# Attention stage: turned values copied out by ScalarE, normalised on GpSimd, with another TensorE order

## The reference, cut to what matters

```python
scores = jnp.einsum('bhqd,bhkd->bhqk', q, k) * d ** (-0.5)
attn = jax.nn.softmax(scores, axis=-1) * (s / np.sqrt(s - 1.0))
out = jnp.einsum('bhqk,bhkd->bhqd', attn, v) * s ** (-0.5)
out = jnp.transpose(out, (0, 2, 1, 3)).reshape(b, s, hid)
return out @ w_o.T * hid ** (-0.5)
```

## Time and profile before

| | us |
|---|---|
| median of three runs | 6009.92 (6009.81 to 6016.19) |
| the profiled execution's own time | 6003.23 |
| its span in the trace | 6001.4 |
| attention stage: first product, last normalised pair | 2146.2, 5009.6 |
| loop of 128 pairs, one pair | 22.05 |

### The profile page before, as it was taken

One profiled execution on the slowest core, in us unless ns is written; L12 is line 12 of the kernel. 1 busy time (PEld: TensorE's weight loads), 2 busy tenths in 40 slices (PEclk: granted clock), 3 DMA queues, 4 the chain that ended last, 5 costly groups with the idle time before them and its releaser, 6 DMA issues. The chain is left out here.

```text
span 6001.4 us, 127338 instructions
## 1 busy us (share of the span) xinstructions
PE 5491.4 (92%) x47968; PEld 3697.5 (62%) x47968; DVE 4566.3 (76%) x7538; ACT 3573.0 (60%) x5381; POOL 1569.2 (26%) x2095
## 2 busy tenths in 40 slices
PE   7888846999989979999999999999999996799998
PEld 5666635999977834444444444444444444599998
DVE  6888867555546768888888888888888885756554
ACT  5666633333324547777777777777777776433332
POOL 4666634333320000111111111111111113533332
PEclk9999968999999979999999999999999998899999
DMA  1111194222218921111111111111111112222221
GB/s 49 42 49 49 39 255 123 85 87 84 98 50 295 334 97 44 56 55 57 57 55 56 55 57 58 55 56 55 57 58 55 56 53 89 80 86 87 86 93 52
DMA packets 315519, 495.75 MB, mean 83 GB/s; under 512 B 36314, under 2 KB 221028, under 8 KB 311024
## 3 DMA queue, kind: packets, MB, share of 16 engines
q1 hardware_dynamic: 290544, 425.73, 22.7%
q0 software_dynamic: 24576, 64.56, 3.3%
HBM read 321.82 MB, written 168.82 MB: 82 GB/s over the span
## 5 line engine op out<-in xcount | busy, mean ns | idle before, releaser
L1707 DVE TENSOR_REDUCE at_best<-at_psM 128x2 f32<-128x1024 f32 x2048 | 2409.8, 1219 | 349.3 <-PE at_psM L1751 349.1
L1663 ACT ACTIVATE at_p<-at_psE 128x1024 f32<-128x1024 f32 (+1 forms) x2688 | 2067.9, 819 | 597.5 <-PE at_psE L1767 561.0
L1767 PE MATMUL at_psE<-at_q,at_k 50*128 50x512 f32 x4096 | 1128.4, 428 | 84.8 <-ACT at_p L1663 83.3
L1751 PE MATMUL at_psM<-at_k,at_q 48*128 48x512 f32 x4096 | 1100.1, 455 | 47.5 <-DMA at_v<-scratch_v 26.4
L1777 PE MATMUL at_psO<-at_p,at_v 128*17 128x256 f32 x16384 | 1089.3, 384 | 0.0
L1767 PEld LDWEIGHTS at_psE<-at_q,at_k 50*128 50x128 f32 x4096 | 559.3, 186 | 493.7 <-ACT at_p L1663 246.8
L1088 ACT ACTIVATE e_h_hi<-e_psH 128x512 fp32r<-128x512 f32 x512 | 306.5, 599 | 919.7 <-PE e_psH L90 771.6
L1162 DVE SCALAR_TENSOR_TENSOR e_h_lo<-e_psH,e_h_hi 128x512 fp32r<-128x512 f32 x512 | 353.8, 691 | 601.6 <-ACT e_h_hi L1088 532.5
L1777 PEld LDWEIGHTS at_psO<-at_p,at_v 128*17 128x17 f32 x16384 | 378.0, 97 | 560.5 <-issue 329.3
L1751 PEld LDWEIGHTS at_psM<-at_k,at_q 48*128 48x128 f32 x4096 | 495.1, 187 | 361.0 <-DVE at_best L1707 171.5
L90 PE MATMUL e_psE<-e_w_hi,e_h_hi 128*128 128x256 f32 x2048 | 582.8, 285 | 0.0
(11 more groups left out here) (202 smaller groups left out, 8548.2 us busy)
## 6 DMA issues: line engine op xcount, KB each, us to landing
e_w_raw<-in_w SPq DMA_DIRECT2D x64, 1024.0 KB
scratch_qk<-cp_qkh SPq DMA_DIRECT2D x64, 512.0 KB
scratch_qk<-cp_qkl SPq DMA_DIRECT2D x64, 512.0 KB
at_q<-scratch_qk SPq DMA_DIRECT2D x256, 128.0 KB
at_k<-scratch_qk SPq DMA_DIRECT2D x256, 128.0 KB
scratch_v<-cp_va SPq DMA_DIRECT2D x32, 544.0 KB
at_v<-scratch_v SPq DMA_DIRECT2D x128, 136.0 KB
a_x<-in_x SPq DMA_DIRECT2D x32, 512.0 KB
```

The costliest lines, as they stand in the source:

```text
L1663: nc.scalar.activation(P[:, u:u + n, :], src, ACT.Exp, scale=HD ** -0.5).then_inc(p_ready, 1)
L1707: nc.vector.reduce_max(best[j % 2][:, h, :, qt], psM[h][:], AX_X).then_inc(m_taken, 1)
L1751: last = nc.tensor.matmul(psM[h][:, a, :], Q[j][r, 128 * qt:128 * qt + 128], K[j][r, 512 * h:512 * h + 512], start=True, stop=True)
L1767: last = nc.tensor.matmul(psE[:, u - u0 if n == 2 else 2, :], K[j][r, 128 * kc:128 * kc + 128], Q[j][r, 512 * half:512 * half + 512], star ...
```

## The change

- ScalarE copies the transposed `psO` to a new SBUF tile `TV` (`take_turned`), before the exponential of group 8. `take_values` moves from before group 4 to before group 6.
- VectorE only inverts the sums, from `TV`, behind query unit 8 (`inverse_sums`); before, it inverted and multiplied from PSUM behind unit 5.
- GpSimd multiplies `TV` by the inverses into `O` (`normalise`), between `add_x` and `split_max`.
- Value block 0 waits for `tv_ready` in place of `o_ready`.
- On TensorE most query units stand one place later, and units 14 and 15 stand behind value block 5. The order of keys and values, `turn_values`, `output()` and `turns()` is the same. At the end `project_out` of one slice stands before the last `turn_values`.

The diff, with most of the unchanged lines left out:

```diff
@@ -1458,6 +1458,7 @@
         rden = sb("rden", [128, 2, KC], F32)
+        TV = sb("tv", [128, 2, KC, 32], F32)
         O = sb("o", [128, KC, D], F32)
@@ -1481,7 +1482,7 @@
         xo_done, xo_taken, xo_hi_ready, xo_lo_ready = sem("xo_done"), sem("xo_taken"), sem("xo_hi_ready"), sem("xo_lo_ready")
-        values_clear = sem("values_clear")
+        values_clear, tv_ready = sem("values_clear"), sem("tv_ready")
         wo_done, y_scaled, y_ready = sem("wo_done"), sem("y_scaled"), sem("y_ready")
@@ -1491,7 +1492,7 @@
         LEAD = 6
-        OUT_AT, MAX_AT, VALUES_AT, NORM_AT = 9, 13, 4, 5
+        OUT_AT, MAX_AT, VALUES_AT, NORM_AT = 9, 13, 6, 8
@@ -1626,18 +1627,30 @@
+            def normalise(p, pb, b):
+                pool.wait_ge(rden_ready, p + 1)
+                if pb % 4 == 0:
+                    after(pool, xo_taken, PB * b + pb - 4)
+                T.settle(pool)
+                nc.gpsimd.tensor_tensor(O[:, :, 32 * pb:32 * pb + 32].rearrange("p t (a d) -> p a t d", a=2), TV[:, :, :, 0:HD],
+                                        rden[:].unsqueeze(3).broadcast_to([128, 2, KC, HD]), ALU.mult).then_inc(o_ready, 1)
             split_max(0, 0, 0)
...
                     add_x(u, ub, n)
+                if not first(pp):
+                    normalise(pp - 1, (pb - 1) % PB, b if pb > 0 else b - 1)
                 if there(pp + 1):
...
             batches(pair)
+            normalise(NP - 1, PB - 1, B - 1)
             for m in range(4):
@@ -1667,6 +1680,11 @@
+            def take_turned(p):
+                act.wait_ge(t_done, p + 1)
+                after(act, o_ready, p)
+                nc.scalar.activation(TV[:], psO[:].rearrange("p (a t w) -> p a t w", a=2, t=KC), ACT.Copy).then_inc(tv_ready, 1)
             def take_out(u, slot, bank):
@@ -1683,6 +1701,8 @@
                         take_values(pp - 1)
+                    if g == NORM_AT and not first(pp):
+                        take_turned(pp - 1)
                     if g == OUT_AT and has_out(pp):
@@ -1693,6 +1713,7 @@
             take_values(NP - 1)
+            take_turned(NP - 1)
             for m in range(4):
@@ -1711,16 +1732,11 @@
-            def normalise(p, pb, b):
-                dve.wait_ge(t_done, p + 1)
-                tv = psO[:].rearrange("p (a t w) -> p a t w", a=2, t=KC)
-                nc.vector.reciprocal(rden[:], tv[:, :, :, HD]).then_inc(rden_ready, 1)
-                dve.wait_ge(rden_ready, p + 1)
-                if pb % 4 == 0:
-                    after(dve, xo_taken, PB * b + pb - 4)
-                nc.vector.tensor_tensor(O[:, :, 32 * pb:32 * pb + 32].rearrange("p t (a d) -> p a t d", a=2), tv[:, :, :, 0:HD],
-                                        rden[:].unsqueeze(3).broadcast_to([128, 2, KC, HD]), ALU.mult).then_inc(o_ready, 1)
+            def inverse_sums(p):
+                dve.wait_ge(tv_ready, p + 1)
+                after(dve, o_ready, p)
+                nc.vector.reciprocal(rden[:], TV[:, :, :, HD]).then_inc(rden_ready, 1)
@@ -1734,10 +1750,10 @@
                             maximum(mp, j, qt, h)
-                        if 2 * i + h == NORM_AT and not first(pp):
-                            normalise(pp - 1, (pb - 1) % PB, b if pb > 0 else b - 1)
+                        if 2 * i + h == 8 and not first(pp):
+                            inverse_sums(pp - 1)
             batches(pair)
-            normalise(NP - 1, PB - 1, B - 1)
+            inverse_sums(NP - 1)
@@ -1771,7 +1787,7 @@
                 if kc == 0:
-                    after(pe, o_ready, pp)
+                    after(pe, tv_ready, pp)
                 for a in range(2):
@@ -1846,26 +1862,27 @@
-                key(0), query(0, 0), key(1), last_values(6)
-                key(2), query(1, 2), key(3), last_values(7)
-                query(2, 3), key(4), key(5), query(3, 5), key(6), query(4, 6), key(7)
+                key(0), key(1), last_values(6)
+                key(2), query(0, 2), key(3), last_values(7)
+                key(4), query(1, 4), key(5), query(2, 5), key(6), query(3, 6), key(7)
                 if not first(pp):
                     turn_values(pp - 1)
-                query(5, 7), key(8), output(), query(6, 8), query(7, 8), key(9), key(10), values(pp, pb % 4, 0)
-                key(11), query(8, 11), key(12), query(9, 12), turns(), values(pp, pb % 4, 1)
-                query(10, 12), key(13), key(14), values(pp, pb % 4, 2)
-                query(11, 14), key(15), query(12, 15), key(16), values(pp, pb % 4, 3)
-                key(17), query(13, 17), key(18), values(pp, pb % 4, 4)
-                key(19), query(14, 19), key(20), query(15, 20), values(pp, pb % 4, 5)
+                query(4, 7), key(8), output(), query(5, 8), query(6, 8), key(9), key(10), values(pp, pb % 4, 0)
+                key(11), query(7, 11), key(12), query(8, 12), turns(), values(pp, pb % 4, 1)
+                query(9, 12), key(13), key(14), values(pp, pb % 4, 2)
+                query(10, 14), key(15), query(11, 15), key(16), values(pp, pb % 4, 3)
+                key(17), query(12, 17), key(18), values(pp, pb % 4, 4)
+                key(19), query(13, 19), key(20), values(pp, pb % 4, 5)
+                query(14, 20), query(15, 20)
             batches(pair)
...
                 values(NP - 1, (NP - 1) % 4, kc)
+            pe.wait_ge(p_ready, NG * NP)
+            project_out(B - 2, PB - 1, psE[:, 0, :])
             turn_values(NP - 1)
             pe.wait_ge(m_taken, 16 * NP)
-            pe.wait_ge(p_ready, NG * NP)
             for m in range(4):
                 turn_out(1, m, NP, psM[m // 2][:, m % 2, :])
-            project_out(B - 2, PB - 1, psE[:, 0, :])
             for n in range(PB):
...
```

## The result

The changed kernel takes 6156.28 us (median, 6152.04 to 6161.65), against 6009.86 for the kernel before in the same comparison: a ratio of 1.0242, 95% interval 1.0224 to 1.0260. That is 146 us more. Predicted were 6127, so 117 more, in a range from 6065 to 6185. The profiled execution took 6161.65.

The account below looks back on a forecast made before the run. TensorE leads, held up by ScalarE and VectorE for 8.74 us of each pair and full for 13.31. Terms -6 + 96 + 26 + 1 = +117 on the profiled 6003.2 give 6120, as median 6127; range 6065 to 6185.

Parts of the forecast that it names:

- The steady pair changes by -0.05 us: Attention's plain pair: earlier k4 and lighter VectorE offset the added ScalarE copy; -0.05 us a pair, -6 us over 120 pairs.
- TensorE stands 3.1 us for `O`, 31 times, +96: At turn_out in every fourth turn, `O` is ready at 11.7 us but asked for at 8.7; +96 us in all.
- The clock falls behind half of them, +26: Behind the 31 waits for `O`, half are followed by a half-rate clock costing 1.65 us each; +26 us, ends 0 and 51.
- The second stretch gives nothing back, and the row transfers are in time: The pair's last 13.31 us, filled by TensorE, recovers no lost time; split_max's later transfers, last issued near 14.6, cost nothing.
- The end, +1: Behind the last pair, take_turned, handoffs and GpSimd lengthen the chain and the moved project_out gives some back; +1 us.
- ScalarE becomes the bound (17%): Rival, 17%: in every pair's first stretch the uncovered take_turned delays exponentials 8 to 12 by 0.49 us; 6163 to 6192 us.
- Faster (7%): Rival, 7%: moved units and lighter VectorE free TensorE's first-stretch holds, 1.2 us a pair, the `O` wait staying; 5981 us.
- `O` isn't late (6%): Rival, 6%: VectorE reaches the inverse before TensorE reaches turns(), so the wait is gone; 6005 us, no change.
- A plain pair of 22.0 us and one of 25 to 27 in every four: Sign expected in the profile after: plain pairs of 22.0 us, with one of 25 to 27 in every four.

## Why the prediction was right, and where it was off

- *The steady pair changes by -0.05 us.* It did: 21.98 to 22.00 against 22.04 to 22.05. In the plain pair shown, counted from 3520.07 (forecast in brackets): k6 1.62 (1.63), take_values 1.94 (1.95), turn_values 2.72 (2.64), take_turned 3.80 (3.85), exponential 8 at 4.27 (4.35), scale_y 5.18 (5.27), unit 6 5.67 (5.6), k9 6.01 (5.95), k12 8.00 (7.95), turns() 8.74 (8.7). A walk through four engines, with durations and handoffs from one traced pair, held to 0.1 us.
- *TensorE stands 3.1 us for `O`, 31 times, +96.* It stood 3.02 us, 31 times, 93.7. GpSimd's product took 0.62 and not 0.73, and started 0.43 behind the inverse's start. By the factor of two in the Trainium skill ("GPSIMD Engine Reference", section 4.1, Engine selection) it would have been 0.85, an estimate; this pass, with both inputs in SBUF against VectorE's one in PSUM, is 1.46 times VectorE's 424 ns.
- *The clock falls behind half of them, +26.* **This is the term that was mis-sized.** It fell behind every wait that was looked at (28 of 28), and the share was 1 in place of 0.5. From 92.66 - 88.17 = 4.49 us per four turns, less the wait's 3.03 and plus the 0.2 that the plain pairs gained, 1.7 is left for one fall, against the forecast price of 1.65. Over 31 waits that is some 52 us, the upper end that the forecast named (51), and not 26. That the price fits so well is luck: it is the mean of 24 falls of 3.4 us, which cost 1.5 each, and four of 6.8 us, which cost 2.8. Why those four lasted longer no run shows. Filling the wait took 61 us away, waiting and all else kept.
- *The second stretch gives nothing back, and the row transfers are in time.* Both held: the last transfer was issued at 14.56 of the plain pair (forecast 14.6), with no wait of TensorE for them, and the run without the wait for `O` is level with the kernel before.
- *The end, +1.* It cost more in the profiled execution. The distance to the kernel before grew from 146.9 us at the last waiting turn to 160.9 at the last pair's product, with the clock at 0.66 over 5150 to 5172 where before it was 1.00. From the same turn to the same product the distance grew by 0.3 to 17 us in the other runs that end as the changed kernel does, and by 3 and 12 in the two that end as the kernel before. So the 14 need not come from the change's own end; this wasn't tested apart.
- *The sum, for the profiled execution* (+158.5 in span): 4.0 before the attention starts, 17.3 up to the 13th turn (three waits, 8.8; the rest fits the clock, which was at half rate for 17 us more than before), 28 times 4.49 = 125.6, 14.0 at the end, -2.4 behind the attention. In medians it is 146, since the profiled execution of the changed kernel was 5 us above its median and that of before 7 below.
- *ScalarE becomes the bound (17%).* It didn't in this kernel: the plain pair shows it, and the added copy was free in the order of before. But it was nearer than the case said: with VectorE's hold out of the way, k9 hung on scale_y at the same moment.
- *Faster (7%)* kept the wait for `O` and needed 0.97 us a pair from lighter VectorE; the plain pair gave 0.05. *`O` isn't late (6%)* fell with the first row of the waits.
- *A plain pair of 22.0 us and one of 25 to 27 in every four* named the turns wrongly in part: the turn with the wait took 25.0, and the fall of the clock came in the turn behind it, 23.5.

## What to carry to other kernels

When an instruction moves to another engine, follow its result to every reader: here one reader in four turns needed it in the same turn, and the average load of the engines said nothing of that. The place at which the first link stands in an in-order queue counted for more than the speed of the engine that got the work: GpSimd's product was 0.2 us longer than VectorE's, but the inverse three units earlier took 140 us away. If TensorE must stand for long, reckon a fall of the clock behind each wait (here all of the waits of 3.0 us and half of those of 1.9), or give it products that nobody reads; and look for a place where an added instruction falls into its engine's own wait.

## What the runs showed of the hardware

- The granted clock fell behind 28 of 28 waits of 3.0 us, behind 15 of 28 waits of 1.9 us, and behind none of 28 when 13 idle products stood in the 3.0 us. Of the falls behind the waits of 3.0 us, 24 lasted 3.4 us at half rate and cost about 1.5 us each, and four lasted 6.8 us and cost about 2.8, in a stretch that TensorE fills.
- It also fell without a long wait, every seventh turn, in a kernel whose plain turn is 22.06 us, and not in those of 21.76, 21.99 and 22.05 us. What the waits of the one have that the others lack was not settled.
- The 128x512 copy from PSUM took 645 ns at its median before exponential 8, against 597 at its shortest, and in the run that stands it behind scale_y 590 ns in the pair shown. The exponential behind it was 1.09 against 1.03. In the changed kernel nothing hung on it.
